# The shared expert's up product made a phase ahead, in one product with the affinities

## The chip, the cores and the metric

The kernel runs on one core of a Trainium2 chip. The metric is the time of the device for one execution, in microseconds. Three runs of the kernel before gave 776.26, 777.49 and 778.57 us; the median is 777.49.

## The reference

The model is a block on 8 batches of 512 tokens, 128 wide, all in 32-bit floats. `x + 0.5 FFN(LN(x))`, then `x + attention(LN(x))`, then `x + 0.5 FFN(LN(x))` with the same weights. The feed-forward part is a mixture of 64 experts, 64 wide, of which 8 count for each token, and one shared expert:

```python
shared = _silu(xf @ Ws_up) @ Ws_down
aff = xf @ centroids.T
_, idx = jax.lax.top_k(aff + expert_biases, TOP_K)
w = _sigmoid(jnp.take_along_axis(aff, idx, axis=1))
w = w / (jnp.sum(w, axis=-1, keepdims=True) + 1e-08)
cw = jnp.zeros((T, E)).at[jnp.arange(T)[:, None], idx].add(w)
h = _silu(jnp.einsum('td,edf->etf', xf, W_up))
routed = jnp.einsum('etd,te->td', jnp.einsum('etf,efd->etd', h, W_down), cw)
return shared + routed
```

The "attention" has no softmax: `xf = u WB'` and `xb = u WBf'` for neighbouring tokens, a gate `gamma = sigmoid(xf w1 + xb w2 + b)`, and `gamma (xf + xb) + (1 - gamma) u`.

## The kernel before

All experts are computed for all tokens, and the weights `cw` (zero for those not chosen) are multiplied in between. The 16 feed-forward passes (8 batches, two each) are 16 phases, numbered 0 to 15. A phase works on one batch: 512 tokens lie along the free dimension, and the 64 experts of 64 hidden values make 32 tiles of 128 rows. Tile 0 is the shared expert. Phases 1, 3, 5 ... are odd and 2, 4, 6 ... even; a hardware loop of five passes holds the odd phases 3 to 11 (`AT_STEADY_A`) and the even phases 4 to 12 (`AT_STEADY_B`), the other phases are written out.

A phase has 35 slots. In slot t the engines do, each in its own order:

- TensorE: the down product of tile t - 6 into `y_ps` (in slots 0 to 5 that of the phase before), then the up product of tile t into `up[t % 5]`. For precision every operand is split in a high and a low part of 32-bit "r" type, so a tile costs three matmuls of 512 columns up and three down (lines 979 to 981, `split_product`).
- ScalarE: silu of tile t in place (L591), then the high part of tile t - 1 into `g_hi` (L625).
- VectorE: tile t times `cw` (L833, `gate`: odd tiles to `gated`, even ones in place), and in odd slots the low part of the even tile before (L842).
- GpSimd: in even slots the low part of the odd tile before (L415).

TensorE may write bank t % 5 of `up` again only when the tile that was in it is gated (odd) or has its low part (even), which `free_bank` waits for. It may make the down product of a tile only when its low part is there.

Beside the tiles every phase prepares others: the layernorms (statistics and `shift` on VectorE, the power -0.5 on GpSimd, the normalisation on ScalarE or VectorE), turning the normed rows (packing in 16-bit halves by GpSimd, L422, a DMA transpose on SyncE's queue, joining the halves by GpSimd), the split of x into `x_hi` and `x_lo` (GpSimd), the affinities, top-k and weights of the next phase, the attention, the copy of `y_ps` (L638) and its turn. The table of each kind of phase says in which slot a step is put on its engine; within a slot the order is that of the code. Each engine works in order, so a step whose operand is late holds back all behind it. SyncE's queue is also in order: a transfer that waits holds the next ones back.

The parts that matter here:

- Affinities (L997, `affinity_blocks`): four plain 32-bit matmuls of 128 tokens by 64 centroids, which the chip runs as eight passes, into `side1`; tokens lie on the rows, so VectorE's bias (L783), max, replace, select and sum follow directly.
- The shared expert. Up product (L1052 and L1053, `up_product` with t = 0): the high and the low weights stand side by side in `su_both`, so rows 0 to 63 and 64 to 127 of the result must be added: ScalarE moves the upper half (L597, `move_shared`), VectorE adds (L852), ScalarE makes silu of 64 rows (L601) and the high part (L605), VectorE the low part into rows 64 to 127 of `g_hi` (L847). Its down product takes two matmuls (L1064, L1065).

## Time and profile before

| | |
|---|---|
| median of the runs | 777.49 us |
| profiled execution | 776.51 us, of which 774.7 us from the first to the last instruction |
| TensorE, matmuls | 764.2 us busy, 99% |
| VectorE | 630.8 us, 81% |
| ScalarE | 629.0 us, 81% |
| GpSimd | 526.2 us, 68% |
| DMA | 28 GB/s on average, 10.7% of the 16 engines' time in the main queue |
| TensorE's granted clock | full in all slices |

A busy share tells how long instructions of an engine were under way. Matmuls overlap, so how fast TensorE gets on is seen in the distance between the starts of two matmuls, not in their durations; likewise on ScalarE and VectorE, where a step from start to start is up to 0.1 us shorter than a duration. "idle before <- releaser" is time in which an engine waited, and whom for.

### The profile page before, as it was taken

To read this page: it belongs to the slowest core of one execution; us is meant where nothing else is said; L and a number is where in the kernel's file an instruction comes from. 1 tells how busy PE (TensorE), PEld (TensorE's weight loads), DVE (VectorE), ACT (ScalarE), POOL (GpSimd) and SP (SyncE) were. 2 spreads that over 40 slices of the span, in tenths; PEclk is the share of its full clock that TensorE was granted. 3 is DMA by queue.
4 is the path that set the end of the run, shared out by engine and by line. 5 is a ranking of instruction groups with operands and counts; after the bars stand their busy time and mean duration, and the time that the engine had idled before them with its cause. 6 is when DMAs were issued, how large, how long until landed. Compare 5 with 4: busy or idle time off the path is not lost.

```text
span 774.7 us, 12422 instructions
## 1 busy us (share of the span) xinstructions
PE 764.2 (99%) x3509; PEld 630.0 (81%) x3509; DVE 630.8 (81%) x1388; ACT 629.0 (81%) x1222; POOL 526.2 (68%) x534
## 2 busy tenths in 40 slices
PE   7999999999999999999999999999999999999998
PEld 6777877888888888888888888888888888888786
DVE  6787989888797787977979788887888788797875
ACT  7987777787887888878888679887788887786885
POOL 4785655676778776776777678776786776564453
PEclk9999999999999999999999999999999999999999
DMA  8000000010101101002010021011110110100000
GB/s 291 15 1 14 15 1 1 14 41 28 28 15 28 41 27 41 14 14 59 22 27 14 16 65 27 14 27 27 40 27 14 27 28 27 14 1 1 14 1 14
DMA packets 56541, 21.99 MB, mean 28 GB/s; under 512 B 42816, under 2 KB 55360, under 8 KB 56512
## 3 DMA queue, kind: packets, MB, share of 16 engines
q1 hardware_dynamic: 56512, 21.64, 10.7%
q8 instruction: 14, 0.23, 0.1%
q14 instruction: 15, 0.12, 0.1%
HBM read 9.05 MB, written 2.10 MB: 14 GB/s over the span
## 4 chain that ended last, share of the span: by engine, by line
PE 89%; DVE 4%; ACT 4%; POOL 1%; issue 0%; DVEq 0%
PE y_ps L979 14%; PE y_ps L981 14%; PE y_ps L980 14%; PE up L979 14%; PE up L981 14%; PE up L980 14%; PE side L997 2%; ACT g_hi L625 1%; ACT up L591 1%; PE side L1030 1%; PE side L1029 1%; POOL g_lo L415 1%; PE y_ps L975 1%; DVE gated L833 1%; DVE up L833 1%; DVE g_lo L842 1%
## 5 line engine op out<-in xcount | busy, mean ns | idle before, releaser
L415 POOL TENSOR_TENSOR g_lo<-gated,g_hi 128x512 fp32r<-128x512 f32 x256 | 333.9, 1305 | 190.8 <-ACT g_hi L625 189.8
L591 ACT ACTIVATE up<-up 128x512 f32<-128x512 f32 x513 | 300.4, 586 | 61.9 <-PE up L981 60.1
L833 DVE TENSOR_TENSOR gated<-up,cw 128x512 f32<-128x512 f32 x256 | 175.7, 686 | 82.4 <-ACT up L591 73.4
L979 PE MATMUL y_ps<-g_hi,wd_hi 128*128 128x512 f32 x512 | 202.4, 395 | 1.6 <-POOL g_lo L415 1.6
L979 PE MATMUL up<-x_hi,wu_hi 128*128 128x512 f32 x512 | 200.2, 391 | 1.0 <-DVE g_lo L842 0.9
L981 PE MATMUL y_ps<-g_hi,wd_lo 128*128 128x512 f32 x512 | 199.6, 390 | 0.0
L981 PE MATMUL up<-x_hi,wu_lo 128*128 128x512 f32 x512 | 199.4, 390 | 0.0
L980 PE MATMUL y_ps<-g_lo,wd_hi 128*128 128x512 f32 x512 | 199.4, 389 | 0.0
L980 PE MATMUL up<-x_lo,wu_hi 128*128 128x512 f32 x512 | 199.4, 389 | 0.0
L833 DVE TENSOR_TENSOR up<-up,cw 128x512 f32<-128x512 f32 x256 | 176.7, 690 | 20.1 <-ACT up L591 18.1
L625 ACT CAST g_hi<-up 128x512 fp32r<-128x512 f32 x256 | 150.6, 588 | 46.5 <-DVE up L833 45.8
L842 DVE TENSOR_TENSOR g_lo<-up,g_hi 128x512 fp32r<-128x512 f32 x256 | 174.6, 682 | 11.3 <-ACT g_hi L625 10.5
L625 ACT CAST g_hi<-gated 128x512 fp32r<-128x512 f32 x256 | 156.1, 610 | 7.3 <-DVE gated L833 7.1
L979 PEld LDWEIGHTS up<-x_hi,wu_hi 128*128 128x128 f32 x512 | 96.1, 188 | 23.0 <-DVE g_lo L842 1.3
L979 PEld LDWEIGHTS y_ps<-g_hi,wd_hi 128*128 128x128 f32 x512 | 96.2, 188 | 22.3 <-POOL g_lo L415 2.4
L981 PEld LDWEIGHTS up<-x_hi,wu_lo 128*128 128x128 f32 x512 | 96.1, 188 | 20.5
L981 PEld LDWEIGHTS y_ps<-g_hi,wd_lo 128*128 128x128 f32 x512 | 96.1, 188 | 20.4
L980 PEld LDWEIGHTS up<-x_lo,wu_hi 128*128 128x128 f32 x512 | 96.1, 188 | 19.9
L980 PEld LDWEIGHTS y_ps<-g_lo,wd_hi 128*128 128x128 f32 x512 | 96.2, 188 | 18.8
L422 POOL COPY n_halves<-normed 128x512 uint16<-128x512 uint16 x34 | 21.8, 652 | 16.5 <-DVE normed L774 9.0
L402 POOL TENSOR_TENSOR rstd<-var_eps,neg_half 128x4 f32<-128x4 f32 x24 | 24.9, 1038 | 2.0
L408 POOL TENSOR_TENSOR x_lo<-x_raw,x_hi 128x512 fp32r<-128x512 f32 x15 | 19.4, 1294 | 1.2
(141 smaller groups left out, 558.8 us busy)
## 6 DMA issues: line engine op xcount, KB each, us to landing
x_in<-in_x SPq DMA_DIRECT2D x8, 256.0 KB, 2.7
wu_raw<-in_w_up SPq DMA_DIRECT2D x4, 512.0 KB, 7.9
wd_raw<-in_w_down SPq DMA_DIRECT2D x4, 512.0 KB, 8.6
x_res<-in_x SPq DMA_DIRECT2D x8, 256.0 KB, 2.6
out<-out_sb SPq DMA_DIRECT2D x7, 256.0 KB, 2.2
mix<-in_mix SPq DMA_DIRECT2D x1, 389.0 KB, 7.3
n_turned_halves<-n_halves SPq DMA_TRANSPOSE x17, 2.7
out<-out_sb SPq DMA_DIRECT2D x2, 128.0 KB, 1.9
```

The lines of the kernel that those rows point to most:

```text
L402: nc.gpsimd.tensor_tensor(rstd[k][:, :], var_eps[k][:, :], neg_half[:, :], ALU.pow).then_inc(rstd_done[k], 1)
L408: nc.gpsimd.tensor_tensor(x_lo[q][:, :], x_raw[:, :], x_hi[q][:, :].bitcast(fp32), ALU.subtract).then_inc(x_lo_done[q], 1)
L415: nc.gpsimd.tensor_tensor(g_lo[:, i, :], gated[:, t // 2 % ORING, :], g_hi[:, i, :].bitcast(fp32), ALU.subtract).then_inc(lo_done[1], 1)
L422: last = nc.gpsimd.tensor_copy(halves[:, h, :, :], words_of)
L591: nc.scalar.activation(up[i][:, :], up[i][:, :], ACT.Silu).then_inc(silu_done, 1)
L625: nc.scalar.copy(g_hi[:, t % GRING, :], src).then_inc(hi_done, 1)
L833: nc.vector.tensor_tensor(gated[:, t // 2 % ORING, :] if t % 2 else up[i][:, :], up[i][:, :], cw[ph.q][:, :], ALU.mult).then_inc(gate_done, 1)
L842: nc.vector.tensor_tensor(g_lo[:, i, :], up[t % RING][:, :], g_hi[:, i, :].bitcast(fp32), ALU.subtract).then_inc(lo_done[0], 1)
L979: nc.tensor.matmul(o, a[0], b[0], start=start, stop=False)
L980: nc.tensor.matmul(o, a[0], b[1], start=False, stop=False)
L981: return nc.tensor.matmul(o, a[1], b[0], start=False, stop=stop)
L997: last = nc.tensor.matmul(aff[:, m, :], rows(x_raw, m), ce_raw[:, :], start=True, stop=True)
```

## The change

For phases 3 to 14 the up product of the shared expert is made in the phase before, together with the affinities of the same tokens. `both_hi` and `both_lo` hold the 64 columns of `Ws_up` beside the 64 centroids, split like all weights; `shared_and_affinities` makes one product of three matmuls into `side1`. Rows 0 to 63 are then the shared expert's input to silu, rows 64 to 127 the affinities, with tokens along the free dimension. ScalarE packs the affinities in 16-bit halves (`aff_pack`), SyncE turns them by a DMA transpose (`turn_aff`), GpSimd joins them to `aff_rows` (`join_aff`), from where the bias and the sigmoid read. ScalarE makes silu and the high part (`silu_ahead`, `high_ahead`), VectorE the low part (`low_ahead`), into a tile of its own, `g_shared`. At the start of phases 3 to 14 slot 0 has no up product, and the move, the add, the silu, the high and the low part of the shared expert are gone from there. Phases 0 to 2 and 15 make the shared expert's product as before; the affinities of phases 1, 2 (made in phases 0 and 1), and of phase 15 are also as before.

The slots of other steps change too: in an odd phase of the loop the next batch's statistics go from slots 16 and 17 to 9 and 10, the split of x from 17 to 7, top-k from 13 to 15, the sum into the output from 11 to 17, and more; in an even one the split of x from 9 to 1, the affinities from 5 to 4, the bias from 7 to 10.

```diff
 AT_STEADY_B = {
-    "x_split": 9, "aff": 5, "sig": 8, "bias": 7, "max": 11, "take": 11,
+    "x_split": 1, "aff": 4, "aff_pack": 4, "sh_silu": 5, "sh_high": 6, "sh_low": 9, "aff_join": 9,
+    "sig": 10, "bias": 10, "max": 11, "take": 11, "gate": 12, "sum": 12, "inv": 15, "cw_pack": (18, 20), "cw_join": (27, 28),
...
+            def turn_aff(p):
+                hold(sp, aff_packed, p - 1)
+                sp.dma_start(a_turned[:, :, :, :].rearrange("p h n e -> p (h n) e"), a_halves.rearrange("p h t -> p (h t)"),
+                             transpose=True).then_inc(aff_moved, 16)
...
                 load_x(c + 1)
+                turn_aff(2 * c - 1)
                 store(c - 2)
...
                 turn_y(2 * c)
+                turn_aff(2 * c)
                 turn_u(c)
...
+            def join_aff(ph):
+                hold(pool, aff_moved, 16 * (ph.p - 1))
+                for h in range(2):
+                    made = nc.gpsimd.tensor_copy(blocks_of(aff_rows[:, :, :], h), a_turned[:, h, :, :])
+                made.then_inc(aff_done[1 - ph.q], 1)
...
+            def aff_pack(ph):
+                act.wait_ge(sh_up_done, ph.p + 2)
+                nc.scalar.copy(a_halves, side1[F:P, :].bitcast(u16).rearrange("p (t h) -> p h t", h=2)).then_inc(aff_packed, 1)
+
+            def silu_ahead(ph):
+                nc.scalar.activation(side1[0:F, :], side1[0:F, :], ACT.Silu).then_inc(sh_silu_done, 1)
+
+            def high_ahead(ph):
+                act.wait_ge(sh_silu_done, ph.p + 2)
+                act.wait_ge(down_done, NT * ph.p + 1)
+                nc.scalar.mul(g_shared[0:F, :], side1[0:F, :], 0.5).then_inc(sh_hi_done, 1)
...
                 elif t == 0:
-                    move_shared(ph)
+                    if not ph.early:
+                        move_shared(ph)
                 else:
                     silu(ph, t)
-                    if t == 1:
+                    if t == 1 and not ph.early:
                         silu_shared(ph)
                         high_shared(ph)
...
-            def add_bias(q, n):
+            def add_bias(q, n, affinities):
                 dve.wait_ge(aff_done[q], n + 1)
-                nc.vector.tensor_tensor(biased[:, :, :], aff, bias_b[:, :].unsqueeze(1).to_broadcast([P, NB, E]),
+                nc.vector.tensor_tensor(biased[:, :, :], affinities, bias_b[:, :].unsqueeze(1).to_broadcast([P, NB, E]),
                                         ALU.add).then_inc(bias_done[q], 1)
...
+            def low_ahead(ph):
+                dve.wait_ge(sh_hi_done, ph.p + 2)
+                nc.vector.scalar_tensor_tensor(g_shared[F:P, :], side1[0:F, :], 0.5, g_shared[0:F, :].bitcast(fp32),
+                                               ALU.mult, ALU.subtract).then_inc(sh_lo_done, 1)
...
+            def shared_and_affinities(ph):
+
+                q = 1 - ph.q
+                pe.wait_ge(both_done, 4)
+                pe.wait_ge(x_lo_done[q], ph.prep[0] + 1)
+                pe.wait_ge(sh_lo_done, ph.p + 1)
+                if not isinstance(ph.p, int) or ph.p > 2:
+                    pe.wait_ge(aff_packed, ph.p - 2)
+                split_product(side1, (both_hi[:, :], both_lo[:, :]), (x_hi[q][:, :], x_lo[q][:, :]), True, True).then_inc(sh_up_done, 1)
...
-                    if t < NT and before(t - RING)[1] < NT and not (ph.first and t < RING):
+                    if ph.early and t == RING:
+
+                        free_bank(ph, -RING)
+                    elif t < NT and before(t - RING)[1] < NT and not (ph.first and t < RING) and not (ph.early and t == 0):
                         free_bank(ph, t - RING)
-                    if t < NT:
+                    if t < NT and not (ph.early and t == 0):
                         up_product(ph, t)
...
                     if ph.at.get("aff") == t:
-                        affinities(q, ph.prep[0])
+                        if ph.early_next:
+                            shared_and_affinities(ph)
+                        else:
+                            affinities(q, ph.prep[0])
```

What the tables make of the order is seen in two places, both in the even phase of the loop.

ScalarE from the first instruction of the even phase to the copy of y, before (`sh_low` is the moved half of the shared expert's product, `up` the tiles; the "ISA" and "REGISTER_ALU" rows set up waits):

```order
L595 ISA
L597 COPY sh_low<-up 64x512
L590 REGISTER_ALU
L591 ACTIVATE up<-up 128x512
L601 ACTIVATE up<-up 64x512
L605 ACTIVATE g_hi<-up 64x512
L590 REGISTER_ALU
L591 ACTIVATE up<-up 128x512
L623 ISA
L625 CAST g_hi<-gated 128x512
L638 COPY y_sb<-y_ps 128x1024
```

ScalarE in the even phase now, from the high part of tile 3 (slot 4) to the high part of the shared expert (slot 6); between the phase's start and the copy of y only two silus and one cast stand, and behind that copy silu 3, high part 2 and silu 4 come ahead of these rows:

```order
L690 CAST g_hi<-gated 128x512
L618 REGISTER_ALU
L619 COPY sh_low<-side 64x1024
L651 REGISTER_ALU
L652 ACTIVATE up<-up 128x512
L690 CAST g_hi<-up 128x512
L622 ACTIVATE side<-side 64x512
L651 REGISTER_ALU
L652 ACTIVATE up<-up 128x512
L690 CAST g_hi<-gated 128x512
L626 REGISTER_ALU
L627 ACTIVATE g_shared<-side 64x512
```

Three instructions of 64 rows went from ahead of the copy of y; three others of 64 rows, one of them with 1,024 values per row, now stand behind it, ahead of the silu of tile 7.

VectorE in the even phase before, from the low part of tile 6 (slot 7) to slot 9:

```order
L842 TENSOR_TENSOR g_lo<-up,g_hi 128x512
L783 TENSOR_TENSOR biased<-side,route 128x256
L912 REGISTER_ALU
L913 SCALAR_TENSOR_TENSOR x<-x,x_res 128x512
L832 REGISTER_ALU
L833 TENSOR_TENSOR up<-up,cw 128x512
L761 BN_STATS stats<-x 128x6 x2
L832 REGISTER_ALU
L833 TENSOR_TENSOR gated<-up,cw 128x512
L842 TENSOR_TENSOR g_lo<-up,g_hi 128x512
```

VectorE there now, from slot 8 (the gate of tile 8) to the bias in slot 10; the row ahead of these is `x<-x,x_res`, which follows the low part of tile 6 directly:

```order
L908 TENSOR_TENSOR up<-up,cw 128x512
L837 BN_STATS stats<-x 128x6 x2
L927 REGISTER_ALU
L928 SCALAR_TENSOR_TENSOR g_shared<-side,g_shared 64x512
L907 REGISTER_ALU
L908 TENSOR_TENSOR gated<-up,cw 128x512
L917 TENSOR_TENSOR g_lo<-up,g_hi 128x512
L837 BN_STATS stats<-x 128x6 x2
L907 REGISTER_ALU
L908 TENSOR_TENSOR up<-up,cw 128x512
L844 BN_AGGR mv<-stats 128x2 x4
L859 TENSOR_TENSOR biased<-aff_rows,route 128x256
```

The bias went from ahead of `x<-x,x_res` (x1) to slot 10, and the low part of the shared expert was put in ahead of the gate of tile 9. Max, replace, select and sum stand in slots 11 and 12 as before, the shift in slot 13.

## Rows read from the trace of the kernel before

**Rows 1.** The page's part 1: busy time, share of the span, instructions.

```profile
PE 764.2 (99%) x3509; PEld 630.0 (81%) x3509; DVE 630.8 (81%) x1388; ACT 629.0 (81%) x1222; POOL 526.2 (68%) x534
```

**Rows 2.** Timeline of TensorE, start of phase 8: start, duration (us), line, operands.

```profile
392.83 0.39 PE L1052 MATMUL up<-x_hi,su_both 128*128 128x512 f32 x1
...
393.29 0.39 PE L979 MATMUL y_ps<-g_hi,wd_hi 128*128 128x512 f32 x1
...
398.73 1.00 PE L997 MATMUL side<-route,x_raw 128*128 128x64 f32 x8
399.54 0.48 PE L1064 MATMUL y_ps<-g_hi,sm_hi 128*128 128x512 f32 x1
```

**Rows 3.** Timeline of VectorE, phase 8, slots 7 to 13.

```profile
403.02 0.69 DVE L833 TENSOR_TENSOR gated<-up,cw 128x512 f32<-128x512 f32 x1
403.62 0.68 DVE L842 TENSOR_TENSOR g_lo<-up,g_hi 128x512 fp32r<-128x512 f32 x1
404.22 0.41 DVE L783 TENSOR_TENSOR biased<-side,route 128x256 f32<-128x256 f32 x1
404.73 0.69 DVE L913 SCALAR_TENSOR_TENSOR x<-x,x_res 128x512 f32<-128x512 f32 x1
...
413.61 0.68 DVE L842 TENSOR_TENSOR g_lo<-up,g_hi 128x512 fp32r<-128x512 f32 x1
414.21 0.15 DVE L903 SCALAR_TENSOR_TENSOR shift<-mv,rstd 128x4 f32<-128x4 f32 x1
```

**Rows 4.** Timeline of TensorE, phase 8: up product 17 and the attention.

```profile
415.08 0.39 PE L979 MATMUL up<-x_hi,wu_hi 128*128 128x512 f32 x1
...
426.64 0.39 PE L1029 MATMUL side<-mix,u_mid 128*128 128x130 f32 x2
```

**Rows 5.** Timeline of ScalarE, phase 8: the first half of the normalisation.

```profile
414.40 0.88 ACT L702 ACTIVATE normed<-x,shift,rstd 128x128 f32<-128x128 f32 x2
```

**Rows 6.** Timeline of GpSimd, phase 8: the last copy of the join.

```profile
426.26 0.19 POOL L461 COPY e<-n_turned_halves 128x2 uint16<-128x2 uint16 x1
```

**Rows 7.** Timeline of TensorE, phase 9: the affinities and what follows.

```profile
453.15 1.00 PE L997 MATMUL side<-route,x_raw 128*128 128x64 f32 x8
453.96 0.48 PE L979 MATMUL y_ps<-g_hi,wd_hi 128*128 128x512 f32 x1
454.27 0.39 PE L980 MATMUL y_ps<-g_lo,wd_hi 128*128 128x512 f32 x1
```

**Rows 8.** Timeline of ScalarE, phase 8, slots 1 to 7.

```profile
395.93 0.59 ACT L605 ACTIVATE g_hi<-up 64x512 fp32r<-64x512 f32 x1
396.42 0.58 ACT L591 ACTIVATE up<-up 128x512 f32<-128x512 f32 x1
...
397.44 1.00 ACT L638 COPY y_sb<-y_ps 128x1024 uint16<-128x1024 uint16 x1
398.35 0.58 ACT L591 ACTIVATE up<-up 128x512 f32<-128x512 f32 x1
...
402.39 0.59 ACT L591 ACTIVATE up<-up 128x512 f32<-128x512 f32 x1
```

**Rows 9.** Busy time by stretch: length, then VectorE's busy time and instructions, granted clock.

```profile
404.73:414.21 9.48, 9.30 (x32) 1.00 0.00 0
```

**Rows 10.** Timeline of ScalarE, phase 9, slot 11, with the idle time before it.

```profile
455.63 0.58 ACT L591 ACTIVATE up<-up 128x512 f32<-128x512 f32 x1 [1.16 <-PE up L981]
```

**Rows 11.** Timeline of VectorE, phase 2: the low part of tile 12.

```profile
133.58 0.68 DVE L842 TENSOR_TENSOR g_lo<-up,g_hi 128x512 fp32r<-128x512 f32 x1
```

**Rows 12.** Timeline of TensorE, phase 2: up product 17.

```profile
134.99 0.39 PE L979 MATMUL up<-x_hi,wu_hi 128*128 128x512 f32 x1
```

**Rows 13.** The page's part 6: DMA issues, the last number us to landing.

```profile
n_turned_halves<-n_halves SPq DMA_TRANSPOSE x17, 2.7
```

**Rows 14.** Groups by line: GpSimd's joins of 512 values; busy us, mean ns.

```profile
L440 POOL COPY cw<-cw_turned_halves 128x512 uint16<-128x512 uint16 x24 | 18.5, 772 | 0.0
```

**Rows 15.** All of VectorE's selects: duration ns min/median/max.

```profile
L803 DVE SCALAR_TENSOR_TENSOR w_sel<-taken,sig x16: 415/742/1075, 11.8 to 720.1; 128x256 f32<-128x256 f32 x16
```

More of the change, by code:

```diff
@@ L88 @@
 AT_THIRD = {
-    "x_split": 3, "aff": 7, "sig": 9, "bias": 8, "max": 9, "take": 9,
-    "gate": 9, "sum": 9, "inv": 15, "cw_pack": (17, 21), "cw_join": (25, 27),
+    "x_split": 3, "aff": 8, "aff_pack": 8, "sh_silu": 9, "sh_high": 10, "sh_low": 11, "aff_join": 11,
+    "sig": 12, "bias": 11, "max": 12, "take": 12, "gate": 12, "sum": 12, "inv": 15, "cw_pack": (17, 21), "cw_join": (25, 27),
     "y_t": 6, "x1": 8, "stat1": (10, 12), "aggr1": 13, "rstd1": 14, "norm1": (16, 18), "xu": 19, "u_t": 22,
@@ L269, in low_count @@
             back, t = before(t)
-            return NLOW[t % 2] * (ph.p - back) + t // 2 + 1
+            return NLOW * (ph.p - back) + (t + 1) // 2
         def halves(ph, name, t):
@@ L289, in rows, with moved @@
             return ap[:, n * P:(n + 1) * P]
+        def moved(ph):
+            return min(ph.p, 3)
         def words(ap, h):
@@ L442, in join_weights, with join_x @@
                     made.then_inc(cw_done[q], 1)
-            def join_x(q, h, moved, value, splits, routed):
+            def join_aff(ph):
[3 more added lines that the diff above has]
+                made.then_inc(aff_done[1 - ph.q], 1)
+            def join_x(q, h, moved, value, splits, routed=None):
                 if h == 0:
                     hold(pool, x_lo_done[1 - q], splits)
-                    hold(pool, routed, splits)
+                    if routed is not None:
+                        hold(pool, routed, splits)
                     hold(pool, moved, value)
@@ L870, in phase @@
                 for t in range(SLOTS):
-                    if t == 0 and not ph.first:
+                    if t == 0 and not ph.first and not ph.early:
                         add_shared(ph)
                     if t == 1:
-                        if ph.late is not None:
+                        if ph.late is not None and not ph.early:
                             low_part(ph, 0)
                         dve.wait_ge(cw_done[ph.q], ph.use + 1)
-                    if t == 2 and ph.late is None:
+                    if t == 2 and ph.late is None and not ph.early:
                         low_part(ph, 0)
+                    if ph.at.get("sh_low") == t:
+                        low_ahead(ph)
                     if 0 < t < NT:
@@ L904, in phase @@
                                                            ALU.mult, ALU.mult).then_inc(shift_done[k], 1)
-                    for name, step in (("bias", add_bias), ("max", find_top), ("take", take_top), ("gate", select), ("sum", sum_up), ("inv", invert_double if ph.halves_next and not ph.cw_dma else invert)):
+                    if ph.at.get("bias") == t:
+                        add_bias(q, n, aff_rows[:, :, :] if ph.early_next else aff)
+                    for name, step in (("max", find_top), ("take", take_top), ("gate", select), ("sum", sum_up), ("inv", invert_double if ph.halves_next and not ph.cw_dma else invert)):
                         if ph.at.get(name) == t:
@@ L1044, in up_product @@
                     pe.wait_ge(x_lo_done[q], 1)
-                    nc.tensor.matmul(o[:, :], w[0], x_lo[q][:, :], start=False, stop=True).then_inc(up_done, 1)
+                    nc.tensor.matmul(o[:, :], w[0], x_lo[q][:, :], start=False, stop=True).then_inc(sh_up_done, 1)
                 elif t > 0:
@@ L1052, in up_product @@
                     nc.tensor.matmul(o[:, :], su_both[:, :], x_hi[q][:, :], start=True, stop=False)
-                    nc.tensor.matmul(o[:, :], su_high[:, :], x_lo[q][:, :], start=False, stop=True).then_inc(up_done, 1)
+                    nc.tensor.matmul(o[:, :], su_high[:, :], x_lo[q][:, :], start=False, stop=True).then_inc(sh_up_done, 1)
             def down_product(ph, t):
-                made, t = low_count(ph, t), before(t)[1]
-                pe.wait_ge(lo_done[t % 2], made)
+                made, (back, t) = low_count(ph, t), before(t)
                 i = t % GRING
                 if t > 0:
+                    pe.wait_ge(lo_done[t % 2], made)
                     last = split_product(y_ps[:, :], (wd_hi[:, t - 1, :], wd_lo[:, t - 1, :]), (g_hi[:, i, :], g_lo[:, i, :]),
@@ L1062, in down_product @@
                 else:
-                    nc.tensor.matmul(y_ps[:, :], sm_hi[:, SD:SD + D], g_hi[:, i, :], start=True, stop=False)
-                    last = nc.tensor.matmul(y_ps[:, :], sm_lo[:, SD:SD + D], g_hi[:, i, :], start=False, stop=False)
+                    pe.wait_ge(sh_lo_done, ph.p - back + 1)
+                    g = g_shared[:, :] if ph.early else g_hi[:, i, :]
+                    nc.tensor.matmul(y_ps[:, :], sm_hi[:, SD:SD + D], g, start=True, stop=False)
+                    last = nc.tensor.matmul(y_ps[:, :], sm_lo[:, SD:SD + D], g, start=False, stop=False)
                 last.then_inc(down_done, 1)
@@ L1072, in free_bank @@
                     pe.wait_ge(gate_done, NJ * (ph.p - back) + tile)
+                elif tile == 0:
+                    pe.wait_ge(sh_lo_done, ph.p - back + 1)
                 else:
```

100 lines of the change are left out of this document (71 added, 29 removed).

## The prediction

> **What bounds the kernel now.** I read the engines' shares first, then the chip's own order of matmuls, then who comes just in time. TensorE is busy for 99% of the span [rows 1], and in the timeline of its matmuls one follows the next: two 512-column products start 0.46 us apart, so 0.23 us each [rows 2], and the same step holds between nearly all of the 3,072 big ones. So the kernel is a chain of matmuls; leaving some out shortens it only as long as their operands still come in time. That is the second thing to read. In a steady phase ScalarE makes silu and the rounded high part, VectorE the gate and half of the low parts, GpSimd the other half, and each tile's low part must be there when TensorE comes to it five to six slots later. In phase 8 (an even phase, second half of the loop's body) the low part of tile 12 ends at 413.61 + 0.68 = 414.29 us and the up product that needs its bank starts at 415.08 [rows 3, 4]: 0.79 us of cover. The second chain there is the layernorm before the attention: shift on VectorE (414.21), normalisation on ScalarE (414.40), packing on GpSimd, a DMA, the join that ends at 426.26 + 0.19 = 426.45, and the attention's first matmul at 426.64 [rows 3 to 6]. 0.19 us of cover, over a chain in which each step follows the one before closely. That is where an even phase will tear first.
>
> **What goes from TensorE.** Phases 3 to 14 lose the shared expert's own two products: 0.46 us x 12 = 5.5 us [rows 2]. The affinities (eight passes of 64 columns) take 398.73 to 399.54 = 0.81 us, and where a big product follows directly its next step is 0.31 instead of 0.23 (453.96 to 454.27), so 0.89 in an odd phase and 0.81 in an even one, where the step after it is long anyway [rows 2, 7]. Three products of 512 columns take their place, 0.69 us. That is 0.20 us saved in each of the six phases 3, 5 ... 13 and 0.12 in each of 2, 4 ... 12: 1.9 us. Together 7.4 us.
>
> **What it costs the others, by place.** In the order of an even phase (shown above) these instructions change.
> ScalarE, start of the phase: the move, the silu of 64 rows and the cast of 64 rows are gone from before the copy of y. What they free is small, since the copy waits for the last down product: it started at 397.44 and can start between 0 and 0.49 us earlier (the step of the 64-row cast, 395.93 to 396.42); I take 0.2 [rows 8]. After the copy of y, before the silu of tile 7, three new ones stand: packing 64 x 1024 two-byte values out of PSUM, a silu and a scaled cast of 64 rows. No row shows the packing with 64 rows. The nearest is the copy of y, with the same 1024 values per row: 397.44 to 398.35, 0.91 us; if only half the rows counted it would be 0.46. The 64-row cast took as long as a full one (0.49 against 0.50), so rows don't count, and I take 0.91. The two others are 0.5 each. So silu 7, now at 402.39, comes 0.91 + 1.0 - 0.2 = 1.7 us later, at 404.1 [rows 8]. ScalarE has no idle time between 398.35 and 402.39 (eight instructions in 4.04 us) to take it up.
> VectorE behind it: gate 7 started 0.63 after silu 7 [rows 3, 8], so it comes at 404.7, the low part of tile 6 at 405.3 and x1 at 405.9. Before, the bias stood between (404.22) and x1 started at 404.73: x1 is 1.2 us late. From x1 to the shift at 414.21 VectorE has nothing free: 9.48 us, busy for 98% [rows 3, 9]. Into this stretch come the low part of the next phase's shared expert (64 rows, 0.6 us, the step of a full one, 403.02 to 403.62) and the bias that was ahead of it (0.51 us, 404.22 to 404.73). The shift is then late by 1.2 + 0.6 + 0.5 = 2.3 us. VectorE's add and low part that are removed at the phase's start had stood in idle time, and give nothing back here.
> TensorE behind that: up product 17 needs the low part of tile 12, 2.3 late less 0.79 of cover less the 0.12 that TensorE has become quicker in this stretch: a wait of 1.6 us. The attention needs the normalised tile: 2.3 - 0.19 + 0.12 = 2.2 us in all, the first wait included. So 2.2 us in each of the five even phases of the loop (4 to 12): 11 us. Bounds of this term: 0.7 us a phase less if both the packing costs half and the copy of y starts 0.49 earlier (a wait of 1.5 us: 7.5 in all); 0.2 us more if the copy doesn't start earlier (12).
> Odd phases: the new instructions stand at slots 11 to 14, where ScalarE had idled 1.16 us for TensorE [rows 10], and top-k, select and x's split have moved. Laying VectorE's new order against the same steps I find every low part in time, the closest (tile 16, behind max, replace and select) with about 0.25 us. No wait is counted there.
> Phase 2: its low part of tile 12 ended at 134.26, its up product 17 started at 134.99 [rows 11, 12], VectorE full before it. One more instruction of 0.6 leaves 0.1 of the 0.73, and tiles behind it had less; I take a wait of 0.5 us, between 0 and 1.
> DMA and GpSimd: twelve more transposes on SyncE's queue, about 2.7 us to land [rows 13], and twelve joins of two copies of 256 values per row, between 0.2 and 0.77 us each (the latter the row of 512 values) [rows 14]. In the queue the new transpose stands ahead of the store and of x's reload in an odd phase, ahead of u's in an even one; those need it 5 us or more later. In an even phase affinities are packed at about 400 us, back by 404, and wanted by the bias at 410. Hidden, both. If the join came later than the bias, the same 2.2 us term would grow by as much. The split of x moves to slot 1 of the even phase, where GpSimd had been idle, and ends well before the new product wants it.
> Sum, against the profiled execution's own time: 776.51 - 7.4 + 11 + 0.5 = 780.7 us. The shown runs' median is 777.49, 1.0 above that execution; against it the changed kernel comes at 781.7 us, +0.5%.
>
> **A rule that would have it otherwise.** Rows 1 name TensorE as the engine with the highest share. The Trainium skill, "Perfetto Trace Analysis", section "Identifying the Most-Contended Engine", says in effect: find the engine with the highest occupancy and optimize it first. By that alone the 7.4 us are all gain, 770.1 us; it is the first rival below.
> The bias will now read two operands in SBUF, where it read one from PSUM. The select, which also reads two in SBUF, took between 415 and 1075 ns, median 742, with the same shape [rows 15]. The Trainium skill, "SBUF — State Buffer", says of the port pair that VectorE and GpSimd share that it is an exclusive lock: a VectorE instruction with two SBUF inputs and a GpSimd instruction that reads SBUF block each other whole. The spread of rows 15 agrees with it. By it the bias could be 0.3 us longer, 1.5 us over the five even phases; it is in the upper end, not in the sum.
>
> **Rivals.** (1) The cover holds: VectorE's and ScalarE's queues take the additions up, TensorE never waits, only the 7.4 us remain: 770.1. For it: VectorE is 81% busy over the span [rows 1]; nothing requires the waits to be passed on in full. Against it: the back-to-back stretch of rows 9 and 0.19 us at the attention. It decides if the shift comes less than 0.3 us late. This is the one on the other side, faster. (2) Half the lateness: packing 64 rows costs half, ScalarE catches up sooner, gates follow earlier, a wait of about 1.1 us per even phase: 777.5 - 7.4 + 5.5 + 0.5 = 776.1. (3) Odd phases tear too: their 0.25 us at tile 16 is gone with the longer bias or a late join; another 1 us in each of six: 787.7. For it, that three instructions and a DMA round trip stand before their top-k; against it the idle 1.16 us.
>
> **Chances.** Forecast (778.5 to 784.5 as its own range) 0.46; rival 1 0.24; rival 2 0.18; rival 3 0.12. This kernel's measurement tells about 0.3% (2.3 us) from no change. Faster than 775.2: rival 1 and a third of rival 2, 0.30. Within: most of the rest of rival 2 and the forecast's low tail, 0.15. Slower: 0.55. The range reaches to 769.5, to take rival 1's own value in, and to 785.5; beyond are part of rival 3 and the low tail of rival 1.
>
> **What would show it.** After: no matmul on the shared weights from phase 3 on; odd phases 0.66 us shorter than before (0.46 + 0.20), even ones about 1.6 us longer (2.2 - 0.46 - 0.12). TensorE's waits, next to nothing before [rows 1], should show some 8 us at "up from wu_hi" behind VectorE's low part, once or twice per even phase near slot 15 to 17, and some 2 to 3 us behind the attention's input or GpSimd's low parts. The packing should last about 1.0 us, silu 7 should start 6 us instead of 4 after silu 3, and the shift 2.3 us later against the phase's third slot. The forecast is wrong if silu 7 isn't late, if VectorE shows idle time between x1 and the shift, or if even phases come out 0.58 us shorter, as in rival 1.

## The result: slower, and by more than forecast

| | before | after |
|---|---|---|
| median of 4 runs, us | 777.85 | 788.38 |
| lowest and highest | 776.26 to 778.57 | 788.28 to 788.86 |
| first to last instruction, profiled execution | 774.7 | 786.5 |

The ratio is 1.0141, 95% interval [1.0127, 1.0155]: 1.4% slower, some 10.5 us. The two profiled executions are 11.8 us apart, as the one before was among the quicker of its kernel (776.51 us). The forecast was 781.7 us, 4.2 us slower, with a range up to 785.5. The direction was right, the size was not, and the time lies outside the range.

The page of the kernel after, its busy times, its chain and its costliest group, answers to [rows 1]:

```profile
PE 766.5 (97%) x3425; PEld 619.5 (79%) x3425; DVE 629.3 (80%) x1376; ACT 634.8 (81%) x1225; POOL 534.8 (68%) x559
...
PE 61%; DVE 19%; ACT 12%; issue 6%; POOL 1%; DVEq 0%; ACTq 0%
...
L1064 PE MATMUL up<-x_hi,wu_hi 128*128 128x512 f32 x512 | 204.0, 398 | 10.9 <-DVE g_lo L917 10.4
```

There are 84 matmul records fewer, and yet the busy time is 2 us longer: a matmul behind a wait shows 0.50 us in the rows below, one in the stream 0.39. The share of TensorE fell from 99% to 97%. TensorE held 89% of the chain that ended last before, and 61% now; VectorE and ScalarE hold 31%, where they had 8%. TensorE's waits on VectorE, from the view of the waits of the kernel after (us in total, times, longest):

```profile
PE up L1064 <- DVE g_lo L917: 10.4, 22, 1.1
```

**By phase.** The distance between the first up products on the experts' weights gives a phase's length. (The shared expert's product of slot 0 stands ahead of that point, so where it is gone from a phase it shortens the length of the phase before.) For phases 8, 9 and 10 the three rows of TensorE's timeline are, before:

```profile
393.97 0.39 PE L979 MATMUL up<-x_hi,wu_hi 128*128 128x512 f32 x1
...
441.60 0.39 PE L979 MATMUL up<-x_hi,wu_hi 128*128 128x512 f32 x1
...
487.20 0.39 PE L979 MATMUL up<-x_hi,wu_hi 128*128 128x512 f32 x1
```

and after, with all rows of phases 8 and 9 between them that carry an idle time of TensorE:

```profile
399.06 0.39 PE L1064 MATMUL up<-x_hi,wu_hi 128*128 128x512 f32 x1
...
414.94 0.50 PE L1064 MATMUL up<-x_hi,wu_hi 128*128 128x512 f32 x1 [0.31 <-DVE g_lo L917]
...
421.96 0.50 PE L1064 MATMUL up<-x_hi,wu_hi 128*128 128x512 f32 x1 [1.10 <-DVE g_lo L917]
...
448.90 0.39 PE L1064 MATMUL up<-x_hi,wu_hi 128*128 128x512 f32 x1
...
475.65 0.50 PE L1064 MATMUL up<-x_hi,wu_hi 128*128 128x512 f32 x1 [0.30 <-DVE g_lo L917]
...
478.84 0.50 PE L1064 MATMUL up<-x_hi,wu_hi 128*128 128x512 f32 x1 [0.18 <-DVE g_lo L917]
...
494.62 0.39 PE L1064 MATMUL up<-x_hi,wu_hi 128*128 128x512 f32 x1
```

So phase 8 went from 47.63 to 49.84 us, phase 9 from 45.60 to 45.72. Before, neither phase had such a row. The same for the rest:

| phases | before, each | after, each | measured, sum | forecast, sum |
|---|---|---|---|---|
| 4, 6 ... 12 (even, loop) | 47.64 | 49.86 | +11.1 | +8.1 |
| 3, 5 ... 13 (odd) | 45.6 (3: 45.49) | 45.7 (3: 45.76, 13: 45.45) | +0.65 | -4.0 |
| 2 | 50.14 | 50.26 | +0.1 | -0.1 |
| 14 | 49.75 | 49.76 | 0.0 | 0.0 |
| sum | | | +11.8 | +4.1 |

The sum is the difference of the spans. (Phase 0 is left out: its first product comes 0.8 us earlier and its fourth 0.8 later, with a granted clock of 0.72 between 10 and 16 us where it was 1.00 before; phase 1 starts at 62.1 us in both.) So 4.6 us of the miss lie in the odd phases, where the forecast counted no wait, 3.0 in the even ones, where the wait was sized too small, and 0.2 in phase 2.

**Phase 8, where the lateness arises.** ScalarE's timeline after, from the copy of y to silu 7, which answers to [rows 8]:

```profile
402.30 1.02 ACT L703 COPY y_sb<-y_ps 128x1024 uint16<-128x1024 uint16 x1
403.20 0.60 ACT L652 ACTIVATE up<-up 128x512 f32<-128x512 f32 x1
...
405.36 1.01 ACT L619 COPY sh_low<-side 64x1024 uint16<-64x1024 uint16 x1
406.39 0.58 ACT L652 ACTIVATE up<-up 128x512 f32<-128x512 f32 x1
...
407.37 0.59 ACT L622 ACTIVATE side<-side 64x512 f32<-64x512 f32 x1
...
408.87 0.60 ACT L627 ACTIVATE g_shared<-side 64x512 fp32r<-64x512 f32 x1
409.35 0.59 ACT L652 ACTIVATE up<-up 128x512 f32<-128x512 f32 x1
```

The packing of 64 rows takes 1.01 us and 1.03 from start to start, as long as the copy of 128 rows with the same 1,024 values per row. Silu 7 starts 6.15 us behind silu 3 (403.20 to 409.35); before it was 4.04. VectorE's timeline after, phase 8, which answers to [rows 3]:

```profile
409.98 0.69 DVE L908 TENSOR_TENSOR gated<-up,cw 128x512 f32<-128x512 f32 x1 [0.81 <-ACT up L652]
410.58 0.68 DVE L917 TENSOR_TENSOR g_lo<-up,g_hi 128x512 fp32r<-128x512 f32 x1
411.18 0.69 DVE L998 SCALAR_TENSOR_TENSOR x<-x,x_res 128x512 f32<-128x512 f32 x1
...
412.88 0.68 DVE L928 SCALAR_TENSOR_TENSOR g_shared<-side,g_shared 64x512 fp32r<-64x512 f32 x1
...
416.08 0.52 DVE L859 TENSOR_TENSOR biased<-aff_rows,route 128x256 f32<-128x256 f32 x1
...
421.23 0.68 DVE L917 TENSOR_TENSOR g_lo<-up,g_hi 128x512 fp32r<-128x512 f32 x1
421.82 0.15 DVE L986 SCALAR_TENSOR_TENSOR shift<-mv,rstd 128x4 f32<-128x4 f32 x1
```

VectorE has only 0.2 us of idle time in all between the low part of tile 6 and the shift. The low part at 421.23 is that of tile 12: TensorE's up product 17 at 421.96 waits for it. Counted from the start of the phase's slot 3 (396.01 before, 401.10 after), silu 7 is 1.87 us later than before, x1 1.36, the shift 2.52 and the attention's first matmul 2.58.

**Phase 9, where no wait was expected.** VectorE's timeline after:

```profile
467.34 0.68 DVE L928 SCALAR_TENSOR_TENSOR g_shared<-side,g_shared 64x512 fp32r<-64x512 f32 x1
467.95 0.68 DVE L908 TENSOR_TENSOR up<-up,cw 128x512 f32<-128x512 f32 x1
468.66 1.00 DVE L859 TENSOR_TENSOR biased<-aff_rows,route 128x256 f32<-128x256 f32 x1
469.59 0.68 DVE L908 TENSOR_TENSOR gated<-up,cw 128x512 f32<-128x512 f32 x1
...
472.91 1.03 DVE L879 SCALAR_TENSOR_TENSOR w_sel<-taken,sig 128x256 f32<-128x256 f32 x1
...
474.91 0.68 DVE L917 TENSOR_TENSOR g_lo<-up,g_hi 128x512 fp32r<-128x512 f32 x1
```

and GpSimd's in the same stretch:

```profile
468.09 1.29 POOL L438 TENSOR_TENSOR g_lo<-gated,g_hi 128x512 fp32r<-128x512 f32 x1 [0.57 <-ACT g_hi L690]
...
472.37 1.29 POOL L567 TENSOR_TENSOR out_sb<-out_sb,x_kept 128x512 f32<-128x512 f32 x1
```

The bias has two operands in SBUF now, where it had one in PSUM. It starts while GpSimd's low part is under way and ends 0.28 us after that one does (469.38); so does the select (`w_sel`), whose end (473.94) lies 0.28 behind that of GpSimd's sum (`out_sb`, 473.66). Each takes 1.0 us; the same bias from PSUM took 0.42 before. The low part of tile 16 ends at 475.59, and up product 21 starts behind it, at 475.65.

### The profile page after: what moved, and what is told of

It is laid out like the page before. It is cut to its first block, busy times and chain, and to the rows that moved or that the text cites. A ratio compares the mean times of both kernels' runs of the same rounds, so it can differ in the third digit from the quotient of the medians.

```text
span 786.5 us, 11865 instructions
## 1 busy us (share of the span) xinstructions
PE 766.5 (97%) x3425; PEld 619.5 (79%) x3425; DVE 629.3 (80%) x1376; ACT 634.8 (81%) x1225; POOL 534.8 (68%) x559
## 4 chain that ended last, share of the span: by engine, by line
PE 61%; DVE 19%; ACT 12%; issue 6%; POOL 1%; DVEq 0%; ACTq 0%
PE up L1064 10%; PE y_ps L1064 10%; PE y_ps L1066 9%; PE y_ps L1065 9%; PE up L1066 9%; PE up L1065 9%; ACT up L652 5%; ACT g_hi L690 4%; DVE g_lo L917 4%; DVE gated L908 4%; DVE up L908 2%; DVE taken L872 2%; DVE w_sel L879 1%; ACT sh_low L619 1%; DVE biased L859 1%
## 5 line engine op out<-in xcount | busy, mean ns | idle before, releaser
L1064 PE MATMUL up<-x_hi,wu_hi 128*128 128x512 f32 x512 | 204.0, 398 | 10.9 <-DVE g_lo L917 10.4
L917 DVE TENSOR_TENSOR g_lo<-up,g_hi 128x512 fp32r<-128x512 f32 x256 | 174.5, 682 | 10.9 <-ACT g_hi L690 10.5
L480 POOL COPY x_raw<-n_turned_halves 128x512 uint16<-128x512 uint16 x24 | 18.1, 780 | 6.2 <-DMA n_turned_halves<-n_halves 6.2
```

The lines of the kernel that those rows point to most:

```text
L480: made = nc.gpsimd.tensor_copy(words(x_raw[:, :], h), plane(n_turned_halves, h))
L917: nc.vector.tensor_tensor(g_lo[:, i, :], up[t % RING][:, :], g_hi[:, i, :].bitcast(fp32), ALU.subtract).then_inc(lo_done[0], 1)
L1064: nc.tensor.matmul(o, a[0], b[0], start=start, stop=False)
```

## The experiments

Unless said otherwise the edit is made to the kernel after. A kernel's time is a median of 4 to 10 runs, and its ratio is to the kernel before on the same chip, whose median was 776.5 to 777.4 us there. "Less than after" is the distance to 788.38, with about 1 us of uncertainty; the lengths of phases are read from the traces and are finer.

**1. Top-k later in the even phase (topk_later).** In the even phase of the loop, bias, max and the rest go behind the shift.

```diff
-    ... "sig": 10, "bias": 10, "max": 11, "take": 11, "gate": 12, "sum": 12, "inv": 15,
+    ... "sig": 10, "bias": 14, "max": 15, "take": 15, "gate": 16, "sum": 16, "inv": 17,
```

> Even phases of the loop alone: bias at slot 14, max and replace at 15, select and sum at 16, the inverse at 17, all behind the shift of the layernorm in slot 13. Theory A (VectorE's queue ahead of the shift holds the normalisation, and that holds TensorE): 0.5 + 0.73 + 0.79 + 0.6 + 0.34 = 3.0 us leave the stretch ahead of the shift, low part of tile 12 and shift come in time, and the 2.8 us of waits in each of five even phases shrink to about 0.5: 788.4 - 11 = about 777. Rival B (the cover is short at every tile, so moving work only moves the wait to tiles 14 to 18): half of it comes back, 783. Rival C (ScalarE's late silus hold TensorE directly): no change, 788.

Measured: 781.93 us, ratio 1.0064 [1.0046, 1.0081]; 6.4 us less than after. Even phases took 48.5. It lies between theory A (777) and rival B (783), nearer to B: the wait at up product 17 is gone, that at 13 stays and a new one comes at 21. Two rows of VectorE's timeline in phase 8 say why:

```profile
416.55 0.15 DVE L985 SCALAR_TENSOR_TENSOR shift<-mv,rstd 128x4 f32<-128x4 f32 x1
417.22 1.29 DVE L858 TENSOR_TENSOR biased<-aff_rows,route 128x256 f32<-128x256 f32 x1
```

In its new place the bias met a GpSimd instruction again (a low part from 416.94 to 418.23) and took 1.29 us.

**2. The shared low part later (low_later).** `low_ahead` in slot 14 of the even phase, and nothing else.

```diff
-    ... "sh_silu": 5, "sh_high": 6, "sh_low": 9, "aff_join": 9,
+    ... "sh_silu": 5, "sh_high": 6, "sh_low": 14, "aff_join": 9,
```

> Even phases of the loop alone: the low part of the next phase's shared expert on VectorE at slot 14 in place of 9, behind the shift. Theory A: 0.6 to 0.7 us less ahead of the shift in each of five phases, the waits shrink by as much: -3.3 us, 785.1. Rival C (ScalarE's backlog is what counts, VectorE would idle in the place): no change, 788.4.

Measured: 784.66, ratio 1.0098 [1.008, 1.0115]; 3.7 us less, 0.78 in each of the five even phases. Its step had been 0.72.

**3. Half the packing (half_pack).**

```diff
-                nc.scalar.copy(a_halves, side1[F:P, :]...rearrange("p (t h) -> p h t", h=2))
+                nc.scalar.copy(a_halves[:, 1, :], side1[F:P, :]...rearrange("p (t h) -> p h t", h=2)[:, 1, :])
```

> Leaves out the low 16 bits of the affinities: ScalarE packs 64 x 512 two-byte values in place of 64 x 1024, in all of phases 2 to 13. Theory A (ScalarE's three new instructions ahead of the silu of tile 7 make gate 7, and then everything on VectorE up to the shift, late): the packing's step of 1.03 us falls to about 0.55, in even phases the shift is 0.5 us earlier and the waits shrink by it: -2.4 us in five of them; odd phases, where VectorE's own work binds, nothing: 786.0. Rival D (the time is lost in VectorE's additions alone): no change.

Measured: 785.56, ratio 1.0109 [1.0092, 1.0127]; 2.8 us less, 0.42 per even phase and 0.10 per odd one, where nothing was expected. The groups of ScalarE, this kernel:

```profile
L619 ACT COPY sh_low<-side 64x512 uint16<-64x512 uint16 x12 | 7.0, 582 | 0.3
```

Half the values per row take 582 ns instead of 1,009: 0.43 us less on ScalarE, and 0.42 less per even phase. In even phases ScalarE's lateness is passed on one to one, through VectorE.

**4. The bias with one operand in PSUM (bias_psum).**

```diff
-    nc.vector.tensor_tensor(biased, affinities, bias_b[...].to_broadcast([P, NB, E]), ALU.add)
+    nc.vector.tensor_tensor(biased, affinities, bias_b[...].to_broadcast([P, NB, E]) if affinities is aff else side0[:, 0:NB * E]..., ALU.add)
```

> Leaves the expert biases out: the second operand of VectorE's addition is read from a PSUM bank in place of SBUF, the shape is the same. Theory E (the addition with two operands in SBUF waits for GpSimd's low part, 1.00 us instead of 0.42 in odd phases): the addition takes 0.42 us again, the odd phases' waits of 1.0 us (tiles 16 and 18) shrink by 0.5 to 0.6 in each of six, -3.3 us; even phases, where it took 0.52, -0.1 each: 784.5 in all. Rival F (odd phases wait because of the added low part and the moved top-k alone): no change in the odd phases, 788.

Measured: 781.75, ratio 1.0059 [1.004, 1.0078]; 6.6 us less, twice what was expected. Odd phases of the loop went from 45.73 to 44.65 each, phase 13 from 45.45 to 44.65, and TensorE has no idle row left in phase 9; even phases gave 0.14. The groups of VectorE:

```profile
L859 DVE TENSOR_TENSOR biased<-aff_rows,side 128x256 f32<-128x256 f32 x12 | 4.9, 407 | 0.2
...
L879 DVE SCALAR_TENSOR_TENSOR w_sel<-taken,sig 128x256 f32<-128x256 f32 x16 | 7.4, 462 | 0.4
```

against these after:

```profile
L859 DVE TENSOR_TENSOR biased<-aff_rows,route 128x256 f32<-128x256 f32 x12 | 9.1, 755 | 0.2
...
L879 DVE SCALAR_TENSOR_TENSOR w_sel<-taken,sig 128x256 f32<-128x256 f32 x16 | 11.2, 697 | 0.4
```

The bias is shorter, as intended. The select, which was not touched, is shorter too. Rows of phase 9 of this kernel, VectorE's and then GpSimd's:

```profile
468.53 0.42 DVE L879 SCALAR_TENSOR_TENSOR w_sel<-taken,sig 128x256 f32<-128x256 f32 x1
...
469.92 0.68 DVE L917 TENSOR_TENSOR g_lo<-up,g_hi 128x512 fp32r<-128x512 f32 x1
```

```profile
468.57 1.54 POOL L567 TENSOR_TENSOR out_sb<-out_sb,x_kept 128x512 f32<-128x512 f32 x1
```

The select starts 0.04 ahead of GpSimd's sum, where it started 0.54 behind it in the kernel after. It runs in 0.42 us, and it is GpSimd's sum that takes longer, 1.54 instead of 1.29. That is the half of the gain that was not expected.

**5. Both moves in the even phase (both_later).** Edits 1 and 2 together.

> Both moves of the even phase together (the shared low part at slot 14, top-k with bias at 14 to 17). With the top-k moved alone, an even phase still waits 0.58 us at up product 13 and 0.92 at 21. Theory A: the first wait goes with the low part, the second stays, since as much work stands ahead of tile 16: 781.9 - 5 x 0.58 = 779.0. Rival B2 (the two moves take away the same lateness): no better than 781.9.

Measured: 777.59, ratio 1.0006 [0.9996, 1.0016]; 10.8 us less than after. Even phases 47.70, with one wait left, at up product 21.

**6. The biases added by GpSimd (bias_pool).** GpSimd adds them behind its join; VectorE keeps the add only where affinities come as before.

```diff
+                hold(pool, aff_done[1 - ph.q], ph.prep[0] + 1)
+                nc.gpsimd.tensor_tensor(biased[:, :, :], aff_rows[:, :, :], bias_b[:, :]...to_broadcast([P, NB, E]),
+                                        ALU.add).then_inc(bias_done[1 - ph.q], 1)
...
-                    if ph.at.get("bias") == t:
-                        add_bias(q, n, aff_rows[:, :, :] if ph.early_next else aff)
+                    if ph.at.get("bias") == t and not ph.early_next:
+                        add_bias(q, n, aff)
```

> GpSimd adds the expert biases right after its join, VectorE no longer does; everything is computed. Theory E (the addition on VectorE stands against GpSimd's low part for the port): VectorE loses 1.0 us in odd phases and 0.5 in even ones, odd phases come to 44.65 us as with the PSUM operand (from 45.73), even ones lose 0.3 to 0.5 us: 788.4 - 6.4 - 2 = 780.0. Rival G (GpSimd's own chain is full, or the addition there blocks VectorE's low part for longer): 786 or more.

Measured: 780.51, ratio 1.004 [1.0025, 1.0055]; 7.9 us less, with everything computed. Odd phases took 44.65, as in experiment 4, though the select takes 0.68 in phase 9 here; even ones took 49.6. GpSimd takes 0.74 us for the add and had the room.

**7. That, and all three shared steps later in the even phase (bias_pool_later).** Edit 6 with

```diff
-    ... "sh_silu": 5, "sh_high": 6, "sh_low": 9,
+    ... "sh_silu": 8, "sh_high": 10, "sh_low": 14,
```

> As with GpSimd's biases, and in even phases ScalarE's silu and cast of the next shared expert at slots 8 and 10 in place of 5 and 6, VectorE's low part at 14. Theory A: in even phases silu 7 is 1.0 us earlier, the shift 0.7 (low part) + 0.5 (bias) + up to 1.0 earlier than in the changed kernel, of 2.8 us of waits at most 0.6 are left: even phases 47.6 us, odd ones 44.65, in all 788.4 - 6.4 - 5 x 2.2 = 771. Rival H (tearing moves on to the chain of the top-k or to GpSimd): 776 or more.

Measured: 781.87, ratio 1.0059 [1.0038, 1.0081]: 1.4 us slower than experiment 6, where 9 us less was expected. All five even phases took 49.8. Rows of x1 on VectorE and of the low part on GpSimd, phase 8:

```profile
406.76 1.29 POOL L437 TENSOR_TENSOR g_lo<-gated,g_hi 128x512 fp32r<-128x512 f32 x1
...
406.87 1.73 DVE L1000 SCALAR_TENSOR_TENSOR x<-x,x_res 128x512 f32<-128x512 f32 x1 [0.42 <-POOL x L500]
```

x1 came 0.11 us behind the start of GpSimd's low part and took 1.73 us instead of 0.69. What ScalarE's new order had won was given back on VectorE. The row says also that x1 had waited for GpSimd's join of y (`POOL x`): when GpSimd's low part is ready to start by then, GpSimd goes on to it at once and x1 comes second.

**8. TensorE's gain alone (quick_aff).** The kernel before, with one of the four affinity matmuls in phases 2 to 13, nothing added anywhere.

```diff
-                affinity_blocks(range(NB)).then_inc(aff_done[q], 1)
+                affinity_blocks(range(1) if not isinstance(p, int) or 2 <= p <= 2 * B - 3 else range(NB)).then_inc(aff_done[q], 1)
```

> The kernel before with three of four affinity blocks left out in phases 2 to 13, nothing added. This measures what time that TensorE no longer needs is worth where no engine gets more work: 0.61 us less in each of twelve phases. Theory I (the cover holds when TensorE alone is quicker): -7.3 us, 770.1. Rival J (the cover was used up before, each us that TensorE gains comes back as a wait): -3 us or less, 774 or more.

Measured: 776.17, ratio 0.9989 [0.9979, 1.0]. Less work for TensorE and no gain: odd phases of the loop are 0.70 us shorter, even ones 0.86 longer. x1 and GpSimd's low part in phase 8 of this kernel:

```profile
403.65 1.30 POOL L415 TENSOR_TENSOR g_lo<-gated,g_hi 128x512 fp32r<-128x512 f32 x1
...
403.79 1.72 DVE L913 SCALAR_TENSOR_TENSOR x<-x,x_res 128x512 f32<-128x512 f32 x1
```

In the kernel before x1 starts at 404.73 [rows 3], 0.17 us ahead of GpSimd's:

```profile
404.90 1.67 POOL L415 TENSOR_TENSOR g_lo<-gated,g_hi 128x512 fp32r<-128x512 f32 x1 [0.31 <-ACT g_hi L625]
```

There GpSimd's low part waited 0.31 us for ScalarE behind the join, x1 got ahead, VectorE takes 0.69 and GpSimd 1.67. The order turned round, and with it who pays. The price on VectorE is 1.03 us, in the stretch that is nearly without idle time [rows 9].

**9 to 11. The same with x1's second operand in PSUM.** In the even phases of the loop x1 reads `side_rows[0]` instead of `x_res` beside its first operand.

```diff
-    nc.vector.scalar_tensor_tensor(x1, <x1 or side_rows[0]>, <scale>, x_res[:, :, :],
+    nc.vector.scalar_tensor_tensor(x1, <x1 or side_rows[0]>, <scale>, x_res[:, :, :] if isinstance(ph.p, int) else side_rows[0],
```

On the kernel of experiment 8 (quick_aff_psum):

> Leaves out three of four affinity blocks, as in quick_aff, and x1's residual: in the loop's even phases VectorE's x1 reads one operand from PSUM instead of both from SBUF. There x1 took 1.72 us, as it started 0.14 us after a GpSimd low part of 1.30 us, where in the kernel before it started 0.17 us ahead of one and took 0.69. Theory L (the port is taken by whoever starts first, and this ate TensorE's gain): x1 takes 0.69 again, even phases 47.0 instead of 48.5, in all 776.2 - 7.5 = 768.7. Rival M (x1 is long because of something else in this order, such as the join it waits for): 1.7 us again, 776.

On that of experiment 7 (later_psum):

> As bias_pool_later, and leaves x1's residual out by reading PSUM in even phases. Theory L: x1 takes 0.69 instead of 1.73, even phases come from 49.83 to 48.8 or, if what is behind it in rows also follows, 48.0: 781.9 - 5 x 1.0 (to 1.8) = 777 to 773. Rival M: no change, 782.

On the kernel before, as the control (before_psum):

> Control: the kernel before with x1's residual left out in the loop's even phases, the operand from PSUM. x1 won the port there, so theory L expects x1 at 0.69 as before, GpSimd's low part of tile 7 at 1.30 instead of 1.67, and no change in time (777.5), as TensorE didn't wait. Rival: the PSUM operand by itself changes the pace, more than 1 us either way.

| kernel | time | ratio | x1 | even phases |
|---|---|---|---|---|
| quick_aff | 776.17 | 0.9989 [0.9979, 1.0] | 1.72 | 48.5 |
| quick_aff_psum | 771.48 | 0.992 [0.9902, 0.9937] | 0.69 | 47.5 |
| bias_pool_later | 781.87 | 1.0059 [1.0038, 1.0081] | 1.73 | 49.8 |
| later_psum | 776.73 | 0.9992 [0.9981, 1.0003] | 0.69 | 48.8 |
| before | 776.82 | 1 | 0.69 | 47.65 |
| before_psum | 776.96 | 0.9996 [0.9985, 1.0007] | 0.69 | 47.65 |

All three held in sign and place: 1.0 us per even phase where x1 had been long, nothing where it had not; in before_psum GpSimd's low part beside x1 takes 1.29 us instead of 1.67, as expected. (Phase 4 of before_psum took 48.49 in the profiled execution: there GpSimd's join of y waited 1.07 us for its DMA transpose, so x1 came 1.04 us later, though not longer.) On quick_aff the time came 2.8 us above the expected 768.7, since even phases took 47.5 and not 47.0: the even phase has another limit there, which stays open. The instances of x1 in quick_aff and then in quick_aff_psum (ns min/median/max):

```profile
L913 DVE SCALAR_TENSOR_TENSOR x<-x,x_res x5: 1715/1724/1728, 217.0 to 590.6; 128x512 f32<-128x512 f32 x5
```

```profile
L913 DVE SCALAR_TENSOR_TENSOR x<-x,side x5: 686/687/689, 217.2 to 586.8; 128x512 f32<-128x512 f32 x5
```

**12. The repaired change (best).** Edits 5 and 6 together, everything computed.

> The two moves of the even phase (low part of the shared expert at 14, top-k at 15 to 17) and the biases on GpSimd, everything computed. Theory A with E: odd phases 44.65 us as with the biases on GpSimd alone, even ones lose the last 0.7 us at up product 21 too and come to 47.0: 777.5 - 6 x 1.07 - 5 x 0.7 = 767.5. Rival K (with other times on GpSimd's queue, x1 in an even phase starts just after a GpSimd low part and takes 1.7 us instead of 0.7): even phases 48 or more, 772 or more.

Measured: 770.88 (770.74 to 771.07), ratio 0.9912 [0.9895, 0.993]: 0.9% faster than the kernel before, 17.5 us less than after. TensorE's timeline, all idle rows of phases 8 and 9 between the phases' first up products:

```profile
390.92 0.39 PE L1066 MATMUL up<-x_hi,wu_hi 128*128 128x512 f32 x1
...
417.75 0.50 PE L1066 MATMUL up<-x_hi,wu_hi 128*128 128x512 f32 x1 [0.37 <-DVE g_lo L919]
...
438.55 0.39 PE L1066 MATMUL up<-x_hi,wu_hi 128*128 128x512 f32 x1
...
483.20 0.39 PE L1066 MATMUL up<-x_hi,wu_hi 128*128 128x512 f32 x1
```

Even phases took 47.62, odd ones 44.65. The expected 767.5 had even phases at 47.0: the wait at up product 21 was to go, and it stayed at 0.64 us of TensorE's steps, against 0.72 in experiment 5. The gain of this version lies in the odd phases, 0.9 us each against the kernel before; the even ones only break even. The bias on GpSimd belongs to it as much as the new slots: with the slots alone (experiment 5) there was no gain.

## Why the prediction was right in sign and wrong in size

**TensorE's saving: right.** Where nothing waits it can be read directly. An odd phase takes 44.65 (experiments 4, 6, 12). Before it took 45.60; what its long steps (0.28 to 0.34 instead of 0.23) had beyond 0.23 was 0.25 in all, which leaves 45.35. That is 0.70 saved, forecast 0.66, and 0.95 with the long steps, of which the forecast had counted one, for 0.08. An even phase without its gaps: 47.68 - 0.80 = 46.88 in phase 8 of experiment 5, 47.63 - 0.17 = 47.46 before; 0.58 saved, as forecast. The sum at the end of the forecast is 0.1 us off: its four terms make 780.6, not 780.7.

**Packing and ScalarE's lateness: right, a little small.** 64 rows cost as much as 128 with the same 1,024 values per row (1.01 and 1.02 us), and half the values per row cost 0.58 (experiment 3). The step was taken as 0.91 and measured as 1.03; silu 7 was forecast 1.7 late and came 1.87 late.

**VectorE's saturated stretch: right.** x1 was forecast 1.2 late and came 1.36 late; the low part was taken as 0.6 and cost a step of 0.72; the shift was forecast 2.3 late and came 2.52 late. Experiments 1, 2 and 3 take one member each out of the sum, and the time falls each time: 0.78 us per even phase for the low part, 0.42 for 0.43 of packing.

**The even phase's wait: the mechanism right, the size too small.** 2.2 us forecast. The phase became 2.21 longer although TensorE saved 0.58, so 2.8 in all. 2.6 of them stand in TensorE's steps beyond 0.23 us (2.73, against 0.17 before): 0.58 at up product 13 and 1.37 at 17, the rest in small ones up to the attention. The idle time at the up products was forecast as some 8 us; of the 10.4 us in the view of waits 7 are in even phases (0.31 + 1.10 in each), and some 3 in odd ones, where none was forecast. Two things were missing. The first wait comes at tile 13, which the forecast's count had not looked at. And a wait costs more than the idle time that the row shows: at up product 17 the row has 1.10, while the step is 1.49 instead of 0.23 and the next one 0.34 instead of 0.23, which makes 1.37. The five even phases of the loop took 3.0 us more than forecast.

**The odd phases: the step that failed.** It was put so: "every low part in time, the closest (tile 16, behind max, replace and select) with about 0.25 us. No wait is counted there." What a second operand in SBUF can do to the bias stood in [rows 15], and the prediction put a price on it in the even phases alone, outside the sum. Measured in phase 9: the bias 1.00 in place of 0.42, and the select 1.03 (it had been 0.94 there before, in a stretch with idle time around it). The low part of tile 16 ends 26.7 us into the phase, 1.2 later than in experiment 4, where the bias takes 0.58 less and the select 0.61 less. TensorE lost 0.57 us at up product 21 and 0.45 at 23, in place of 0.25 before, and with that all of the 0.70 saved. The forecast's margin itself was sound with a short bias, as an estimate shows: experiment 4 has 0.79 us between the end of that low part (470.60) and up product 21 (471.39), and with the select at the 0.94 of before 0.27 of it would be left. A bias 0.58 longer uses up more than that. Experiment 4 settles it: with one operand in PSUM the odd phases become 1.08 us shorter each in the loop, 6.2 us in all six, of the 7.0 us by which the profiled execution is shorter. Experiment 6 finds the same 44.65 by another way. This is rival 3 of the prediction, at a chance of 0.12. It named the longer bias as what decides. Its price was 1 us in each of six phases, measured are 0.8 (1.02 us of long steps, 0.77 more than before); that its time, 787.7, lies only 0.7 from the one measured owes something to the even phases, which cost more than it assumed.

In the prediction the exclusive lock of the Trainium skill ("SBUF — State Buffer", section "SBUF: two separate sides") stood as 0.3 us in the even phases alone. Its text: of the two, the one that "starts first gets the pair for the whole instruction; the other fully blocks". The runs agree: the bias took 1.00 or 1.29, the select 1.03 and x1 1.73 behind GpSimd, and GpSimd took 1.67 where x1 came first. With x1's second operand in PSUM it takes 0.69 (experiments 9 to 11). Applied to the bias of the odd phases the rule would have shown that the 0.25 us are at risk.

**What else was ruled out.** Rival 1 (the cover holds) needed the shift less than 0.3 us late; it came 2.52 late. Experiment 8 shows besides that TensorE's saving alone, with nothing added elsewhere, is not kept: 776.17 us, where 770.1 was expected if the cover held. Rival 2 needed the packing to cost half; it costs 1.01 us. DMA and join: GpSimd's wait for the turned affinities is 1.3 us over the whole kernel. Phase 2 grew by 0.1 although 0.58 was saved in it, so it had 0.7 us of new waits; 0.5 was taken, between 0 and 1.

**What stays open.** The bias and the select in odd phases were changed together in effect; how much of the 1.08 us each would have cost alone was not separated. By the margin of 0.79 us in experiment 4 either alone (0.58 or 0.61) would leave some 0.2 at up product 21, so it may have taken both; that is an estimate from the rows, not a run. The longer even phases in later_psum (48.8), the rest of quick_aff_psum (47.5) and the wait at up product 21 in the best version were not explained either.

## What to carry to other kernels

Before you put an operand of a VectorE instruction from PSUM into SBUF, look up what GpSimd does at that moment, and count the instruction at both prices: its own, and its own behind a GpSimd instruction that has just started. Lay the changed order out not for the phase that looked tight but for each kind of phase, with those prices, since a margin of 0.25 us is not a margin when one instruction of the stretch can be 0.6 longer. And where all engines run just in time, work taken from the busiest one can be worth next to nothing until the others' work has been moved with it (experiment 8: 0.1%). The same idea made the kernel 1.4% slower with its first table, and 0.9% faster with two steps moved and the bias on GpSimd.

## What the runs showed that was not expected

- How long the second of two colliding instructions takes can be read off to some 0.02 us. With own durations of 1.29 (GpSimd's low part), 0.69 (x1), 0.42 (bias, select) and 0.15 (shift), it ends its own duration less 0.14 us behind the end of the first one: the bias and the select of phase 9 0.28 behind (0.42 - 0.14), x1 in bias_pool_later 0.55 behind (0.69 - 0.14), GpSimd's low part 1.15 behind x1 in the kernel before (1.29 - 0.14). The shift of phase 9 takes 0.93 instead of 0.15 in this way, in the kernel after as in that before. So an instruction that is met in its last 0.14 us costs the other nothing.
- A shift of some 0.3 us between two engines decides about 1 us: x1 0.17 us ahead of GpSimd's low part takes 0.69 us, 0.14 or 0.11 behind it 1.72 to 1.73. The state repeats in every pass of the loop (1,715 to 1,728 ns over five), so it doesn't average out; it moved the time of two kernels by about 5 us each (776.17 to 771.48, 781.87 to 776.73).
- Taking three of four affinity matmuls away (experiment 8) made five phases 0.86 us longer each.
- The length of a ScalarE copy from PSUM goes by the values per row: 64 x 1024 took 1.01 us, 128 x 1024 1.02, 64 x 512 0.58.
